# A two-layer decoder on one core: the causal mask of the self tiles as one 128-row product instead of two 64-row products

## The reference

```python
att = jnp.einsum('bhqd,bhkd->bhqk', q, k) * scale
causal = jnp.tril(jnp.ones((T, T), bool))
att = jnp.where(causal[None, None], att, -jnp.inf)
y = jnp.einsum('bhqk,bhkd->bhqd', jax.nn.softmax(att, axis=-1), v)
...
attc = jnp.einsum('bhqd,bhkd->bhqk', qc, kc) * scale
y = y + jnp.einsum('bhqk,bhkd->bhqd', jax.nn.softmax(attc, axis=-1), vc)
...
return y @ Wp + bp
```

## Time and profile before

| | |
|---|---|
| runs | 810.38, 814.89, 817.66 us; median 814.89 |
| profiled execution | 815.48 us, its span 813.6 us |
| busy share of the span | PE 79%, PEld 43%, DVE 66%, ACT 53%, POOL 19% |
| stage of the two passes | about 71 to 424 us; the steps from about 104 us |
| one unit in the steps | 19.25 us (235.44 to 254.69) |
| mask products (L600) | 256, first at 94.3, last at 422.9 us |

### The profile page before, as it was taken

One profiled execution on the slowest core, in us unless ns is written; L12 is line 12 of the kernel. 1 busy time (PEld: TensorE's weight loads), 2 busy tenths in 40 slices (PEclk: granted clock), 3 DMA queues, 4 the chain that ended last, 5 costly groups with the idle time before them and its releaser, 6 DMA issues. The chain is left out here.

```text
span 813.6 us, 13336 instructions
## 1 busy us (share of the span) xinstructions
PE 641.9 (79%) x5152; PEld 349.2 (43%) x5152; DVE 534.7 (66%) x686; ACT 429.0 (53%) x773; POOL 153.9 (19%) x149
## 2 busy tenths in 40 slices
PE   4985786999989999999886856898701789977996
PEld 2843332333333333333322333686200267754884
DVE  3355985888888888888423369799298344335432
ACT  2553354888888888888880122455733212224323
POOL 7111324432000000000003259000070171003100
PEclk9997876999999999999995669899955769999999
DMA  7142584444111111110012042741000210000000
GB/s 179 39 151 81 175 269 155 141 150 149 56 52 49 49 47 47 47 47 2 2 19 76 1 170 100 198 142 65 0 0 0 79 63 1 1 0 1 1 0 27
DMA packets 32314, 57.58 MB, mean 71 GB/s; under 512 B 6408, under 2 KB 22544, under 8 KB 31808
## 3 DMA queue, kind: packets, MB, share of 16 engines
q1 hardware_dynamic: 28400, 36.89, 14.2%
q0 software_dynamic: 3392, 17.77, 6.6%
q10 hardware_dynamic: 464, 2.12, 1.0%
HBM read 38.18 MB, written 16.49 MB: 67 GB/s over the span
## 5 line engine op out<-in xcount | busy, mean ns | idle before, releaser
L830 ACT ACTIVATE prob<-ps 128x512 f32<-128x512 f32 (+2 forms) x480 | 253.5, 581 | 73.8 <-PE ps L650 65.2
L940 DVE TENSOR_REDUCE pm<-ps 128x2 f32<-128x1024 f32 x192 | 225.9, 1220 | 31.8 <-PE ps L612 29.9
L673 PE MATMUL ps<-prob,vst 128*9 128x256 f32 (+1 forms) x1664 | 131.8, 389 | 18.7 <-ACT o_all L818 17.4
L650 PE MATMUL ps<-qq,kc 50*128 50x256 bf16 (+1 forms) x832 | 135.2, 279 | 8.0 <-DMA qq<-mrow 7.9
L612 PE MATMUL ps<-kc,qq 48*128 48x512 bf16 x384 | 120.1, 403 | 12.0 <-issue 7.5
L650 PEld LDWEIGHTS ps<-qq,kc 50*128 50x128 bf16 (+1 forms) x832 | 52.1, 96 | 103.9 <-ACT prob L830 78.5
L1062 POOL TENSOR_TENSOR y<-y 128x256 f32<-128x256 f32 x16 | 11.4, 721 | 250.5 <-issue 235.9
L673 PEld LDWEIGHTS ps<-prob,vst 128*9 128x9 f32 (+1 forms) x1664 | 25.2, 88 | 63.1 <-ACT prob L830 49.9
L612 PEld LDWEIGHTS ps<-kc,qq 48*128 48x128 bf16 x384 | 33.6, 95 | 20.9 <-DVE pm L940 9.6
L947 DVE TENSOR_REDUCE nm<-ps 128x4 f32<-128x512 f32 (+1 forms) x32 | 30.7, 958 | 16.0 <-PE ps L600 16.0
L1754 ACT ACTIVATE prob<-s 128x512 f32<-128x512 f32 (+1 forms) x28 | 15.5, 567 | 45.0 <-PE s L1692 45.0
(11 more groups left out here) (341 smaller groups left out, 1252.0 us busy)
## 6 DMA issues: line engine op xcount, KB each, us to landing
kc<-kc_scr SPq DMA_DIRECT2D x32, 150.1 KB
comb_bc<-comb_scr SPq DMA_DIRECT2D x8, 512.0 KB, 4.5
kc<-kc_scr SPq DMA_DIRECT2D x32, 100.1 KB
raw<-in_wexp POOLq DMA_DIRECT2D x8, 384.0 KB, 6.1
exp_scr<-raw_high POOLq DMA_DIRECT2D x8, 384.0 KB, 3.3
exp_scr<-raw_low POOLq DMA_DIRECT2D x8, 384.0 KB, 6.2
up_high<-exp_scr SPq DMA_DIRECT2D x8, 256.0 KB, 2.7
up_low<-exp_scr SPq DMA_DIRECT2D x8, 256.0 KB, 2.8
```

The source lines that it names most:

```text
L650: last = pe.matmul(bank[0:p, j * TQ:(j + 1) * TQ], kc[s][rows, j, t * 128:t * 128 + p], qq[s][rows, 0, j, :], start=(j == 0), stop=True, s ...
L673: last = pe.matmul(o_ps[32 * hh:32 * hh + VW, kind * TQ + q0:(kind + 1) * TQ], value[:, hh * VW:(hh + 1) * VW], prob[0:k, (NST * n + t) % ...
L830: act.activation(prob[0:p, g % P_RING, 2 * e:2 * e + 2, q0:TQ], s2[0:p, k % S2_RING, 0:2 * w].rearrange("p (i q) -> p i q", i=2), ACT.Exp, ...
L940: dve.tensor_reduce(pm[:, m % 2, c, :, jt], banks, AX.X, ALU.max).then_inc(s1_read, 1)
```

## The change

`add_mask` issues one product with all 128 rows instead of two with 64. Its weights are the whole identity and its moving operand the whole mask, both in form 0. The columns are the same 256, the target is the same, and `e` no longer matters. The 128 calls now issue 128 products and weight loads where they issued 256. The layout of `masks_b`, and all other code, stays; lines behind L600 move up by two.

```diff
                     def add_mask(o, mask, e):
 
-                        rows = slice(GROUP * e, GROUP * (e + 1))
-                        for half in range(2):
-                            done = pe.matmul(o, ident_b[rows, half, :], mask[rows, half, :].unsqueeze(1).to_broadcast([64, 2, 128]),
-                                             start=False, stop=(half == 1), skip_group_check=True)
+                        done = pe.matmul(o, ident_b[:, 0, :], mask[:, 0, :].unsqueeze(1).to_broadcast([128, 2, 128]),
+                                         start=False, stop=True, skip_group_check=True)
                         return done
```

## The result

| | before | after |
|---|---|---|
| runs, median | 816.27 us (810.38 to 818.61) | 843.67 us (839.79 to 848.16) |
| profiled execution's span | 813.6 us | 837.9 us |
| PE busy in the span | 641.9 us | 674.3 us |
| instructions | 13336 | 13080 |
| one unit of the steps | 19.26 us | 20.95 us |

The ratio is 1.035, with a 95% interval of 1.027 to 1.043. The forecast was 842 us.

The account below looks back on a forecast made before the run. PE was taken to set the pace around the mask products. 14 x 0.99 (halves) + 15 x 0.77 (self tiles) + 0.98 (first units) = 26.4 us on 815.5, so 842 us; range 829 to 852.

Parts of the forecast that it names:

- s = 0.11: Price in us on PE of each change between 64-row and 128-row products.
- u: Time PE takes to stream 256 columns, 0.1075 us; 512 columns are 2u.
- exits cost twice (851): Upper bound: mask phases pay on leaving too, 102 exits x 0.09 = 9.2 us more, 851 us.
- The lengths of the four steps: Added score time: tile 13 3s, tile 14 u + 3s, half 13 u + 4s, half 14 2u + 4s.
- 0.22 us hidden behind half 14: Half 14's last piece, u + s, falls within PE's 0.56 us wait for the maxima; 0.34 stay.
- DVE's two waits: Waits for PE's mask products before the self score reductions: from 0.39 and 0.62 to about 0.9 and 1.0 us.
- The first units: Unit 0's halves 13 and 14, which run ahead, delay unit 1's start by 3u + 6s = 0.98 us.
- The cover of unit 0's steps: Self tiles of unit 0 and halves of unit 1 cost nothing; PE waits 6.3 us after them for DMAs.
- the free switch: Rival: the halves of the rows are tied together but switches cost nothing; 4.9 us more, 820; 8%.
- the strict order: Rival: PE products start strictly in written order; 0.5u a unit less, 815 with free switches; 3%.
- The weight loads as the bound: Rival: loads hold up the mask steps' products, so fewer give back 10.9 us, 804.6; 4%.
- The clock rival: Rival: more gaps lower PE's granted clock from 2.4 to 1.2 GHz; 15 us more, 857; 3%.

Follow-up runs that it names:

- the product of zeros: Kernel before with a 128-row product of 16 columns of zeros added after the scores of context tiles 0 to 11: 829.5 us, 1.019.
- The self tiles alone: Kernel before with the 128-row mask product only in the second pass, self tiles 13 and 14: 825.3 us, ratio 1.012.
- the halves alone: Kernel before with the 128-row mask product only in the first pass, halves 13 and 14: 830.9 us, ratio 1.021.
- tail-first kernel: Changed kernel with pair 1's last second-pass product before the second mask product in the steps of halves 13 and 14: 836.4 us, 1.028 to before.

## Why the prediction was right

The forecast was +26.4 us on 815.5. Measured are 27.4 us between the medians, with an interval of 22 to 35, and 24.3 between the spans of the two profiled executions. Up to the last output product (L673, L671), which starts at 423.98 us before and 450.13 after, the changed kernel lost 26.15 us; what follows took 1.9 us less in this execution, with the same work. The 26.15 come together as follows, from the starts of L639 (before) and L637 (after) in each unit:

| stretch | forecast, us | measured, us |
|---|---|---|
| up to the start of unit 1 (132.51 before, 134.25 after) | 0.98 | 1.74 |
| from there to the first L639 behind it (147.03, 149.21) | 0.99 | 0.44 |
| the next 13 units (to 397.63, 421.71) | 22.9 | 21.9 |
| the last two self tile pairs, to the last output product | 1.54 | 2.07 |

So the mechanism is right, and carries 21.9 of the 26.15 us. That the total is met within 1 us is partly luck: the four deviations, of 0.5 to 1.0 us each, cancel. The 1.0 of the third row is 0.07 us a unit, by which the four steps are shorter than s = 0.11 makes them. Step by step:

- **In work alone nothing is gained.** Right. The halves of the rows ran as separate streams, and the 128-row product takes one stream of both.
- **The switch, s = 0.11.** Right in size and in both directions: pieces of 2u + s and of u + s = 0.215 us stand all through the mask steps. That exits or entries alone cost (831) and that exits cost twice (851) both fall with these pieces. One step was counted without a row that shows it. The prediction defines a switch as a change between 64 and 128 rows and then also counts the boundary between the second mask product and L671, where both sides have 128 rows. By the definition tile 13 would have had 3 of them, 0.98 us; with the boundary there are 4, and 1.08 were measured. It came true, and the product of zeros shows that price by itself.
- **The lengths of the four steps.** Expected 3s, u + 3s, u + 4s, 2u + 4s more, which is 0.33, 0.44, 0.55 and 0.66 us. Measured are 0.32, 0.41, 0.53 and 0.63. The self tiles alone cost 0.74 us a unit (expected 0.77), the halves alone 0.96 (0.99).
- **0.22 us hidden behind half 14.** Right, shown by the tail-first kernel and by the waits.
- **DVE's two waits.** Expected about 0.9 and 1.0 us, measured 0.71 and 1.26. Their sum is right, its parts are not: half 13's last piece, u + s, stands behind the mask product that the first wait ends with, so it belongs to the second wait. By this 0.39 + 3s = 0.72 and 0.62 + 2u + 4s = 1.28.
- **The first units.** Too small, by 0.76 us. SP's wait for the first maxima grew from 0.3 to 1.7 us:

```profile
SPq L375 <- DVE mrow L959: 1.7, 1, 1.7
```

I priced the preparation's masks at the full clock and left out the switch between half 13's last mask product and half 14. In the stretch of the first self scores the granted clock was at the lower level, 1.2 GHz, for nearly all of the time (0.50 of full speed from 94.0 to 97.5 before, 0.53 from 94 to 99 after); in the 3 us before, PE had been busy for 0.92 us before the change and 1.25 after it. A stream costs double there: the step from 134.25 to 135.22 after, at the same level, has four streams and a switch in 0.97 us, and the piece from 95.47 to 95.80 below has one stream and a switch in 0.33, so a stream takes 0.213 us. With 3 of these streams and 7 switches the masks cost 1.4 us, and that is measured: from the first self product to the start of the last mask product 1.3 us passed before (94.18 to 95.5) and 2.68 after (94.52 to 97.20). The other 0.34 us are no part of the change, since the first self product, ahead of any mask, starts that much later (94.18 and 94.52). After:

```profile
94.00:99.00 5.00, 3.62 (x14) 1.04 (x14) 3.00 (x5) 0.00 (x0) 0.00 (x0) 0.53 0.44 122
...
95.47 0.40 PE L598 MATMUL ps<-masks_b 128*128 128x256 bf16 x1
95.80 0.61 PE L621 MATMUL ps<-ks,qq 48*128 48x256 bf16 x2
96.33 0.40 PE L598 MATMUL ps<-masks_b 128*128 128x256 bf16 x1
```

- **The cover of unit 0's steps.** Right. PE's wait for the DMA of maxima, 6.3 us, took up their delay, and had 4.2 left:

```profile
PE ps L648 <- DMA qq<-mrow: 4.2, 1, 4.2
```

- **Behind that wait.** Too large, by 0.55 us. From there to the next L639 the granted clock was 0.68 of full speed on average before and 0.74 after, so the changed kernel had less of the lower level. That this gave the 0.55 us back is likely, but no run shows it alone.
- **The last two units.** Too small, by 0.5 us, and not because of the masks. The two self tile pairs cost 0.65 and 0.50 us (402.74 to 405.13 before against 426.81 to 429.85 after, and 421.32 to 423.98 against 446.97 to 450.13), less than the 0.77 each that I had. The other 0.93 us came in the context tiles between them, which the change doesn't touch:

```profile
405.13:421.32 16.19, 14.19 (x160) 3.70 (x157) 3.04 (x5) 13.67 (x27) 0.00 (x0) 0.89 0.13 20
```

```profile
429.85:446.97 17.12, 15.20 (x160) 3.63 (x156) 3.04 (x5) 13.99 (x27) 0.00 (x0) 0.80 0.12 19
```

Both kernels fell to the lower level there after the copy-out wait, and the changed one stayed at it for longer (0.50 from 433.52 to 438.06). Whether the change made it stay longer is open.

Of the rivals, the free switch fell with all kernels of 128 rows, and the strict order with the earlier trace rows and its counterpart after: before the change, pair 1's products start beside the first mask product, though they are written behind the second; after it they can't. The weight loads as the bound fell with the change itself, which took 128 of them away and got slower by the lengths that streams and switches give. The clock rival fell for the steps: the granted clock was 1.00 of full speed from 150 to 400 us in both kernels. Outside them it was at the lower level for a part of three of the four stretches of the table, which is not in the forecast.

## What to carry to other kernels

Where PE runs 64-row products on both halves of its rows, count the work of each half, and read the price of going over to 128 rows from a place where the trace has it; merging two half-height products into one of full height is no gain if the other half was in use, and each cut costs its switches and the idle rest of the shorter half. Put products of one kind next to each other before asking whether they are fewer. Ask for each piece that is added which wait lies behind it, and at which clock it runs. When a total is met, add it up again by stretches: terms that are off can cancel.

## What was new about the hardware

- A switch costs about 0.11 us in all forms that the mask steps have: from 64 rows into 128-row products with 9 or 128 columns of weights, back from a mask product to 64 rows, and from a 128-row product with 128 columns of weights to one with 9 (0.11 from 253.29 to 253.40, with the 16 columns it streams). The wide f32 product L477 behind 64-row products is an exception in the earlier trace rows: 0.10 on entering, and its first record takes 0.10 more than the next.
- It hardly depends on the clock. At the lower level the mask piece from 95.47 to 95.80 took 0.33 us. One stream of 256 columns takes 0.213 us there, twice u (worked out above from this piece and a step of four streams), so s is about 0.12 us.
- PE's busy share hides it. The changed kernel's PE is busier (80% for 79%) with 128 products fewer; only distances between starts show the price.
